# Other order strings and another bank table for a five-engine transformer kernel

## The reference

```python
x = x + 0.5 * _L0_ffn_ref(_layernorm(x), gate0, up0, down0)      # silu gate, int weights with scales
x = x + _L0_attn_ref(_layernorm(x), Wq, Wk, Wv, Wo)              # 16 heads of 16, rotary, causal
x = x + 0.5 * _L0_ffn_ref(_layernorm(x), gate0, up0, down0)
x = x + 0.5 * _L1_ffn_ref(_layernorm(x), w1, w2, w3)             # ternary weights, sigmoid gate
x = x + _L1_attn_ref(_layernorm(x), Wq, Wkv, Wo, bo)             # 16 query heads, 4 key heads, alibi, causal
x = x + 0.5 * _L1_ffn_ref(_layernorm(x), w1, w2, w3)
```

## Time and profile before

| | |
|---|---|
| runs | 583.16 us median of 3 (582.78 to 583.98) |
| profiled execution | span 584.2 us; no other time of it is listed |
| PE busy | 535.6 us, 92% of the span |
| DVE, ACT, POOL busy | 461.8, 401.5 and 340.4 us |
| mean granted TensorE clock | 0.984 |
| instructions | 12653 |
| DMA | 15.0% of the 16 engines' span on queue 1 |

### The profile page before, as it was taken

How to read it: one execution, slowest core, us unless ns; L and a number is a source line. 1 busy time by engine, 2 the same in 40 slices (tenths; PEclk the granted TensorE clock), 3 DMA queues, 4 the chain that set the end, 5 groups by cost and what they waited for, 6 DMA issues and landing times.

```text
span 584.2 us, 12653 instructions
## 1 busy us (share of the span) xinstructions
PE 535.6 (92%) x4924; PEld 290.7 (50%) x4924; DVE 461.8 (79%) x813; ACT 401.5 (69%) x605; POOL 340.4 (58%) x427
## 2 busy tenths in 40 slices
PE   2887987998999999999899998999999999999987
PEld 1353642544653654655546564465455644553664
DVE  4888979898889789589986878887897767783454
ACT  5866576678577758855687756867769596669433
POOL 2367886864896578844645167624455724437543
PEclk9978997999999999999999999999999999999999
DMA  8700020121022100310210102010211021001301
GB/s 327 311 2 1 22 88 1 55 74 42 20 85 65 37 4 3 121 65 1 77 40 3 47 17 74 22 41 0 69 41 38 4 78 50 22 1 41 111 0 73
DMA packets 19627, 31.73 MB, mean 54 GB/s; under 512 B 6464, under 2 KB 7872, under 8 KB 19416
## 3 DMA queue, kind: packets, MB, share of 16 engines
q1 hardware_dynamic: 19568, 30.93, 15.0%
HBM read 13.75 MB, written 2.36 MB: 28 GB/s over the span
## 4 chain that ended last, share of the span: by engine, by line
PE 57%; DVE 14%; ACT 9%; POOL 7%; issue 7%; DMA 5%; SPq 1%; DVEq 0%; POOLq 0%; ACTq 0%
PE PS L583 17%; PE PS L607 10%; PE PS L694 9%; PE PS L674 4%; DVE MX L1050 4%; PE PS L625 4%; PE PS L659 4%; PE PS L567 3%; ACT PB L838 3%; PE PS L709 3%; DMA RB<-scratch 2%; ACT XN L761 2%; PE PS L539 1%; DVE MX L1046 1%; DVE ST L863 1%
## 5 line engine op out<-in xcount | busy, mean ns | idle before, releaser
L838 ACT ACTIVATE PB<-PS 128x1024 f32<-128x1024 f32 x160 | 158.9, 1024 | 50.3 <-PE PS L674 43.2
L1050 DVE TENSOR_REDUCE MX<-PS 128x2 f16<-128x1024 f32 (+2 forms) x192 | 158.4, 865 | 23.1 <-PE PS L539 22.9
L583 PE MATMUL PS<-XT,WGU 128*128 128x512 f16 x660 | 158.2, 382 | 2.8 <-DVE PB L990 1.1
L1126 POOL TENSOR_TENSOR HH<-TH,HH 128x512 f16<-128x512 f32 x71 | 82.2, 1168 | 86.1 <-ACT HH L806 85.8
L1154 POOL TENSOR_SCALAR_AFFINE_SELECT PB<-PB 128x512 f32<-128x512 f32 (+1 forms) x140 | 73.2, 550 | 53.1 <-ACT PB L838 53.1
L583 PEld LDWEIGHTS PS<-XT,WGU 128*128 128x128 f16 x660 | 59.1, 98 | 74.1 <-issue 5.9
L607 PE MATMUL PS<-WD,HH 128*128 128x256 f16 x660 | 78.0, 273 | 1.1 <-POOL HH L1126 0.6
L694 PE MATMUL PS<-PB,V 128*32 128x512 f32 (+3 forms) x1024 | 75.5, 435 | 1.3 <-POOL PB L1154 1.1
L607 PEld LDWEIGHTS PS<-WD,HH 128*128 128x128 f16 x660 | 62.4, 98 | 14.0 <-issue 3.1
L659 PE MATMUL PS<-SK,SQ 63*128 63x256 f16 (+3 forms) x512 | 60.7, 300 | 6.5 <-DVE MX L1050 3.6
L674 PE MATMUL PS<-SQ,SK 64*128 64x384 f16 (+3 forms) x512 | 58.5, 300 | 8.0 <-ACT PB L838 2.4
(11 more groups left out here) (122 smaller groups left out, 756.4 us busy)
## 6 DMA issues: line engine op xcount, KB each, us to landing
SQ<-QPB SPq DMA_DIRECT2D x24, 256.0 KB, 2.5
OC<-OT SPq DMA_DIRECT2D x16, 256.0 KB, 2.4
RB<-scratch SPq DMA_DIRECT2D x32, 128.0 KB
SK<-QPB SPq DMA_DIRECT2D x12, 256.0 KB, 3.1
SQ<-MT SPq DMA_DIRECT2D x128, 1.0 KB
out<-X SPq DMA_DIRECT2D x8, 256.0 KB, 2.2
PB<-gu SPq DMA_DIRECT2D x2, 704.0 KB, 6.1
X<-x_in SPq DMA_DIRECT2D x2, 512.0 KB, 5.4
```

The source lines that it names most:

```text
L583: m = e.matmul(o[:, :], WGU[l][:, k, col:col + P], rows_of(f)[j][:, k, :], start=j == 0 and k == 0, stop=j == 1 and k == 1)
L838: e.activation(PB[Q % 2][:, j, :, :], two_banks("s", i), ACT.Exp, scale=0.25).then_inc(a_exp, 1)
L1050: e.tensor_reduce(mx[:, :, pr, t], o[:, :, col:col + (t + 1) * P], AX.X, ALU.max, negate=True).then_inc(a_max, 1)
L1126: e.tensor_tensor(hh[1][:, s * T:(s + 1) * T], value_of(j)[0], hh[0][:, s * T:(s + 1) * T], ALU.subtract).then_inc(f_lo, 1)
```

## The change

The dictionary ORDER gets new strings for all five engines and a new string of banks. Each string holds the same letters equally often as before; nothing else differs. Cut to two lines of each sort:

```diff
 ORDER = {
     "sp":
-        "kkrrkrkrDSrRDSRrkrDSRkrrDSRrrDrkSRkDSRrrlkkrDrSRrDSlRrkrkDrSRrDSrRrkkrDrSRDrSRrDkrkSRDrSRrrrDSRDOSOR"
+        "kkkrrrkrrDDSSRRrrkDkSrRrDSrRrkrDlSkDSRRrrrkkrrDrSDSRRlrkkrrDrSDSRRrrkkrDrDSSRRrrDrkkrSRDSrROrrODSDRSR"
         "OOOOOO",
     "pe":
-        "ttggGggGaGgttGGggGggddddGaGgtggGuutGqqddddvqgGgvgqGGGgugugGqttqmmgmgmmmmmqmsqsdsmgGmsdmsdmmsdsmmpmsG"
+        "ttggggGGGGagttgGgGgggGgGddddGgattuuGqqqddddgggqgGvvGGGgGuuqgtqtmmmmgmmmgmqqgssGmdsmdmsdmsmsmdmmspmss"
...
     "banks":
-        "7657247041575464537217560127506743163251703463712537543705126021464265264656210622642062605264062506"
+        "1076015401525407624351640232750614134616732150347065176024706240642165412602562624262606025260462504"
...
 }
```

More of the change, by code:

```diff
@@ new lines @@
+        "smvmmpmGmmGgmgmssmsGmmsmsddttddmspmsgoooossggmsgmsGmmmpsGsGssggssspssGGttpgggdGddgdGGGoggGoooddddttg"
+        "gGGgggGGGgdddd",
+    "dve":
+        "NwNttwhwwhhhwwttkwhhhhNkhwwdwwdhwnhwwuuNhttpqqpdwdhnppqhqhhkhuupqtqhptmmmmmmxssmmhpqpmqmhxdmmsmmmxdm"
+        "mkhmsnmhmxmshmmmmmxsmmmhcmcxmmmuummpxqpqmooNpqpqmdmmttdmxcshsshhnkmsmmmsmmxhhsmmhmmxcmuuddmNppqqmomt"
+        "tomNqxhhpkmmhhmmmxhqhpttsdhcdnksshhcmmmmsssmuxhumohmohmmllmmxmmldmmdmxNmmmmmxttNhkmhhhmmhhmmcxttddnm"
+        "shsmmmkcuussxhhhmmllsslhhmmommxddmNmmmxomttNhhmmhmkcmxhhhmmmmcmxmmmmddmxnmttomuusosshhhklllmmshmsshx"
+        "hmmmmmxdmdmNmmmmxcttcNhhhkmmhhmhmttxddnoommmNmuumcxlhllkhhmmmmmhxmmhmmmhmcxmmtddmtmxhookNmmhmmmxhhht"
+        "tchchhdkdhhhhooNdXdtthhhkhhhdd",
@@ new lines @@
+    "act":
+        "TwwXxxwXttttwwhwhxxtwwhtktthhhhwwtthhXtkkkYyhyhtxxhQXtkQktttvwkYhhtQyyQhhhvxtxThkQQtteeeetQeeQhehoee"
+        "eteeeoetehhhoeeeeteYoeeevveehyyocceeeeeQQXexxoQQeettteehhhetoteeeetYhoeechhvvyyeeceeXoxxQeeeetthhtXt"
+        "tQeeoehheteQhxhxoeeeteeQthotYhhvtttvcycyhhhQeQeeQeeeeeoeeXexxeeeotehtttXhhhttheheoxxeeeettoYhtvyyete"
+        "eQehhcQthtQcehheeoeeeeXoxxeetteetehhhoeeettthhhoeeeveXecceeoeexxYeyytttQhhhQQeetthteehhoeeeeeeoeeeXo"
+        "xxeetttvhhhXtttheehheeexccxYooeyyeetQQQhetteeteeeeoXhhvohtteeehhexxceceeotheetteteXhoeeheetteeeeexxh"
+        "hoohtttchchthhtthhXxxtthhthtthhth",
@@ new lines @@
+        "0427601624162520426426056203740632416204260416254327402652072451264106204561540624164204340624603406"
+        "2402402460246042762146034560234632504621624106306431246024367045702640274562406252042654603406064204"
+        "3604267642072402650246251463064206242074206420724067240673254241714260217624074216240462124626412640"
+        "6205136421063040275060426403264045426052460235042076354621506246025604602460270462406240652416206431"
+        "506324072056024074602762046204731517365367154637032154374260320512",
```

38 lines of the change are left out of this document (10 added, 28 removed).

## The result

| | before | changed |
|---|---|---|
| median of 4 runs | 582.97 us (582.35 to 583.98) | 598.29 us (592.93 to 598.93) |
| ratio to before | | 1.0242, 95% interval [1.0199, 1.0285] |
| span of the profiled execution | 584.2 us | 591.2 us (its own time 592.93) |
| PE busy | 535.6 us | 534.3 us |
| DVE, ACT, POOL busy | 461.8, 401.5, 340.4 us | 460.1, 401.0, 342.8 us |

What follows compares the result with a forecast made beforehand. PE, busy for 535.6 of 584.2 us, was taken as the bound. The terms -2.0 + 0.5 + 0.5 + 2.4 - 3.0 gave -1.6 us, so 582.6 us of span or about 581.6 us median, range 575.5 to 588.0.

Steps and rivals of the forecast that it cites:

- opening: Start of the kernel through the attention unit's transposes: 2.0 us won, between 5.0 won and 1.0 lost.
- `k` ahead of `r`: SP's queue: third `k` ahead of the first `r`, which then waits; 0.5 us lost, between 0 and 2.4.
- both `R` behind the second `D`: Output chains of six of eight attention units: `R` issued later; 0.5 us lost, between 0 and 2.4.
- the middle: From 100 to 560 us: swaps close a sixth of PE's idle time; 3.0 us won, between 6 won and 4 lost.
- end: Behind the last `p`: PE reaches the output projection with less work ahead; 2.4 us lost, between 0 and 3.9.
- the second `R` issues up to 1.14 us later: SP's queue in six attention units: the first `R` now goes just ahead of the second, delaying it by up to 1.14 us.
- the bound of 2.4 us a unit: Output chains: most that the later `R` and POOL's work behind it could cost a unit where nothing covers it, 2.4 us.
- units 3 to 6 are covered: Between last `p` and first `o`: PE's work gives some 4 us or more of cover, so late `R` costs nothing.
- rival 1: Opening gains in full, clock included: -6.6 us, or 576.6 us; chance 0.2.
- Rival 2: Output chains come late through SP's queue and PE's order at the output projection: +3.8, or 587.0 us; chance 0.22.
- Rival 3: DVE's instructions stretch beside POOL's weight work, so the opening loses 1.0 us: +1.4, or 584.6 us; chance 0.08.
- rival 4: New order does nothing that counts: the middle's swaps win and lose alike, the opening's lead is spent; 583.2 us; chance 0.1.

Runs made afterwards that it cites:

- opening alone: Kernel before with the new strings up to the first row maxima on PE, DVE, ACT and POOL, SP as before: 583.54 us, ratio 0.9993.
- tail of before: Changed kernel with all five strings of before from the last attention unit's output chain on: 591.37 us, ratio 1.0146.
- the wide `R`: Each `R` as four DMAs over 32 partitions instead of two over 64: 582.2 us on the kernel before, 586.39 us on the changed kernel.

## Why the prediction was wrong

The sum was -1.6 us; measured is about +14. In terms of the forecast:

| term | forecast | measured, and from what |
|---|---|---|
| opening | -2.0 (-5 to +1) | -0.4, and nothing for certain: opening alone, 0.9993 |
| `k` ahead of `r` | +0.5 (0 to 2.4) | 0 with the new opening: `r` issued at 93.77, before at 94.01 |
| both `R` behind the second `D`, and the middle | +0.5 and -3.0 | +8.5 together: tail of before, 1.0146; the lower clock behind PE's waits is in it; about +1.2 of it is left when `R` is wide |
| end | +2.4 (0 to 3.9) | about +5: 2.2 to 2.4% less 1.46%, and 5.3 in the profiles; 3.3 with the wide `R` |

**The step that failed** is "the second `R` issues up to 1.14 us later", and with it the bound of 2.4 us a unit and the sentence that units 3 to 6 are covered. It took the landing times of before for fixed and counted only what a DMA's issue costs on SP. In the trace of before an `R` mostly runs by itself. In the new order two `R` lie back to back in units 0, 2, 3, 4 and 5, a `D` right behind an `R` in unit 6 and an `S` in unit 7; they need the same four of the sixteen DMA engines, and each lands later by what is left of the one ahead. The second `R` of a pair lands 5.7 to 7.1 us behind its issue (before 4.7 to 5.3), the `D` of unit 6 4.4 instead of 1.9, and the `S` of unit 7 4.05 instead of 1.8. These add up to some 12 us of later landings over the eight units, which is an estimate of what was overlooked and not of the time lost, as PE's work covers part of it. The bound had a second fault: 2.4 us is the price of one unit, and six were changed.

All of it was to be read from the trace of before, in its windows behind an `R`, where the share stands at a quarter. I looked at queues by their issue times alone.

A second thing stood at nothing: the clock. It was in the prediction only as a gain of the opening, in rival 1. Behind waits of PE in the middle and in the tail it falls to the 1.2 GHz level for a while; by the second profile this is some 5 and 1.7 us of a long execution.

**Rival 2 was right in kind.** It named output chains that come late, SP's queue and PE's order, with waits of L709 for the splits, at 0.22. These waits are what the profile after shows. Its price, 587.0 us, was 11 us short, because it was built from the same bounds.

**The end** was right in mechanism: PE comes to L709 with less work ahead, and waits. With the wide `R` the tail from the last `p` to the end is 47.7 us, 2.4 more than the 45.3 of before and 2.9 more than the 44.8 of before with the wide `R`. That this meets the forecast of 2.4 is in part luck, as its parts were other ones: PE waits 1.60 and 0.83 us at L709, not about 2, and 0.34 and 0.21 us between the last transposes and L583, not 1.4. The rest, in the real change, is the `S` held up by an `R`, and 1.5 us of half-speed matmuls behind the wait (4.25 less 2.75). In the change itself these last two waits are also 0.34 and 0.21 us.

**The opening** failed on three points: L935 ends only behind POOL's conversion and takes 2.8 us more, not 0.7, at a place where PE then waits for DVE; the lead at the transposes is spent by the first `p`; and the reference was a long execution, with 1.8 us of its own up to the first `p`. Rival 3 named DVE beside POOL, and the row of L935 bears it out, but without a loss to the end, since only the gain went.

**The middle** had the wrong sign. The reason given, that a search which starts at PE's gaps should close some, was no row of the trace. With the wide `R` the new middle runs level; so its swaps win and lose alike, as rival 4 had it.

Three things stay open: why the clock falls behind a wait of PE in one execution and not in another with nearly the same wait, how the 8.5 us divide among the units, and how they divide between later landings and the lower clock.

## What to carry to other kernels

Price a reordering of DMAs by what will be in flight together, not by issue times: for each DMA read the share of the engines that it holds, and for how long, from windows of one microsecond behind its issue. Here a transfer with four entries in its slowest dimension held up those right behind it; widening it was the only edit here that made the kernel faster (0.44%), and it took most of the penalty off a bad order. A wait of PE can cost more than its length: look at the granted clock behind it, in more than one profile. Order strings of several engines are one solution: undoing SP's string alone gave the slowest kernel of all, undoing PE's tail alone gained nothing, and both told little, so undo a stretch on all engines, and mind the splice.
